# A decoder layer in fp32: three of four query tiles projected and rotated inside the attention steps

## Chip, cores, metric

The kernel runs on one core of one Trainium2 chip. The metric is the device time of one execution in microseconds. The time before is 1650.46 us, the median of 3 runs (1649.22 to 1653.79). Engines are called TensorE (PE, its weight loads PEld), VectorE (DVE), ScalarE (ACT), GpSimd (POOL) and SyncE (SP).

## What is computed

Three sublayers with residuals over x of 4 x 512 x 512, all in fp32. The core of the reference, cut down:

```python
x = x + attn(_layernorm(x), wq, wk, wv, wo, bq, bk, bv)   # 16 heads of 32, 2 kv heads, rope, causal
x = x + mamba(ctx_1024, _layernorm(x), ...)               # scan over 512 steps, 16 states, gated by silu
x = x + ffn(_layernorm(x), Wg, Wu, Wd, Wr, Ag, ...)       # 512 -> 1408 -> 512, top 2 of 8 LoRA experts

q = (x @ wq.T + bq); k = (x @ wk.T + bk); v = (x @ wv.T + bv)
q = apply_rope(q);   k = apply_rope(k)        # [x1*cos - x2*sin, x2*cos + x1*sin]
out = softmax(mask(q @ k.T * scale)) @ v
state = state * exp(d * A) + (d * u) * b      # step of the scan
y = sum_n(state * c)
```

The scan does not need the attention: its input is ctx_1024. Only the gate at its end takes the normalized x.

## The kernel before, in words

The four batches (b, or t for the batch whose feed-forward runs) are worked through one after another, each on one engine program per engine, with semaphores between them. The scan of batch t + 1 is spread over the feed-forward of batch t, the down products of batch t, and the attention of batch t + 1. The order on each engine is written out: `plan` (line 93) lists the scan's 60 pieces on VectorE and which slot each falls into.

For each batch after the first, the slots are: 33 evaluations of the feed-forward (gate and up products, adapters), then 11 slots of the down product, then 32 attention steps (`STEPS`) and four more that only drain. Batch 0 has the 11 slots without down products.

- **Down slot f** on TensorE (lines 970 to 978): 16 matmul records `L974` over the four row tiles, then `project(b, f)`. `projections(f)` (line 131) says what f carries: slots 1 to 5 project the five tiles raw 0 to 4 (0 to 3 are the query tiles of four heads, 4 the keys), slots 2 to 6 rotate them, slot 7 projects the values, slot 8 turns them by transposes.
- **A tile's way**: TensorE projects it with four 128 x 128 by 512 matmuls (each two records in the trace, `L782`) into a bank of `ps_w`; ScalarE adds the bias and moves it to `q_raw[n % 2]` (`L605`), after tile n - 2 has been rotated; TensorE multiplies by a rotation matrix (`L789`); VectorE forms raw * cos + rotated * sin in three operations (`L1105`, `L1108`, `L1112`) and counts `qk_ready`.
- **Attention step s** handles query tile m = s // 8 and row tile i = (s // 2) % 4, two heads of the four. TensorE: scores of s (`L820`, mask `L823`), transposes of the probabilities of s - 2 (`L834`), and at every second step from 5 on the product with the values (`L844`, `L849`). VectorE: maxima (`L1126`), reciprocals, the scan pieces of the step, division (`L1139`). ScalarE: moves of the transposed probabilities (`L637`), exponentials (`L625`), moves of outputs (`L644`), decays for the scan (`L583`). The scores of s wait for the exponentials of s - 2. At steps 31, 33, 34, 35 the output projection `L873` follows.
- **Banks of `ps_w`**: two banks go round by a fixed list of uses (`uses_of`, line 160). `fill` waits until the use before the last is freed.
- **Scan state n**: VectorE multiplies into `state` (`L1086`), scans (`L1091`), multiplies by C (`L1096`); GpSimd then issues a DMA that adds the 1 MB state to y (`L487`), after the add before it has landed. The product of state n waits for the add of state n - 2 (line 1083).
- **Seam**: after the 11 slots VectorE runs `finish` (`L1280`), which empties `ps_a`; the first two scores steps wait for it (`x3_ready`, line 816), and attention waits for all five tiles (line 807).
- **SyncE** loads the context of the next batch after all five tiles of this one are rotated (line 408), then the first weight tiles of the feed-forward.

Of the kernel before, what the change touches and what calls it, by code (L numbers as in the profile page):

```python
# [11 lines left out]
P = 128  # L12
# [118 lines left out]
def projections(f):  # L131


    raw = f - 1 if 1 <= f <= TILES else None
    back = f - 2 if 2 <= f <= TILES + 1 else None
    return raw, back, {TILES + 2: 0, TILES + 3: 1}.get(f)
# [23 lines left out]
def uses_of(first, last):  # L160
# [15 lines left out]
    if not last:  # L176
# [15 lines left out]
def decoder_layer(nc, x, ctx_t, wq, wk, wv, wo, w_in, w_x, w_dt, w_lora, w_r, b_down, a_down, w_tiles, w_adapt, w_down,  # L192
                  vectors, constants, out, bc_rows):
    with ExitStack() as stack:
# [38 lines left out]
        probs_t = [r1[:, 4 + k, :] for k in range(4)] + [xt[:, k, :] for k in range(4)]  # L233
# [3 lines left out]
        r2 = sb("r2", [P, 15, L])  # L237
        k_t, q_t, q_raw, rope_tmp = r2[:, 0, :], r2[:, 8:12, :], r2[:, 12:14, :], r2[:, 14, :]
# [274 lines left out]
        def _(act):  # L513
# [78 lines left out]

            def project(b, f):
                n = projections(f)[0]
                if n is not None:
                    bank = filled(act, ("raw", n), b)
                    if n >= 2:

                        act.wait_ge(qk_ready, b * TILES + n - 1)
                    elif not first_batch(b):  # L600

                        act.wait_ge(down_ready, b)

                    bias = q_bias[:, n:n + 1] if n < MT else vec[:, V_BQ + n:V_BQ + n + 1]
                    nc.scalar.activation(q_raw[:, n % 2, :], ps_w[:, bank, :], ACT.Identity, bias=bias,  # L605
                                         scale=SCALE if n < MT else 1.0).then_inc(work_free[bank], 1)
# [7 lines left out]
            def attention(b, slots):  # L614
# [118 lines left out]
        def _(pe):  # L733
# [39 lines left out]

            def project(b, f):
                raw, back, values = projections(f)
                if raw is not None:
                    if raw == 0:
                        xt_moved("xt", b, False)
                    bank = fill(pe, ("raw", raw), b)
                    for k in range(KT):  # L780
                        w = wq_sb[:, k, raw * P:(raw + 1) * P] if raw < MT else wk_sb[:, k, :]
                        mm = nc.tensor.matmul(ps_w[:, bank, :], w, xt[:, k, :], start=(k == 0), stop=(k == KT - 1))  # L782
                    mm.then_inc(work_full[bank], 1)
                if back is not None:
                    bank = fill(pe, ("back", back), b)

                    raw_bank, raw_count = use(("raw", back), b)
                    pe.wait_ge(work_free[raw_bank], raw_count + 1)
                    nc.tensor.matmul(ps_w[:, bank, :], rot, q_raw[:, back % 2, :], start=True, stop=True)\  # L789
                        .then_inc(work_full[bank], 1)  # L790
# [15 lines left out]
            def attention(b, slots):  # L806
                pe.wait_ge(qk_ready, (b + 1) * TILES)
                pe.wait_ge(v_ready, b + 1)

                def scores(s):  # L810
                    m, i, pair = s // (2 * NT), (s // 2) % NT, s % 2
                    if s >= 2:
# [44 lines left out]
                for s in range(STEPS + 4):  # L857
                    if s < STEPS:
                        scores(s)
                    if 2 <= s < STEPS + 2:  # L860
                        transpose_probs(s - 2)
                    for g in value_groups(s):
# [149 lines left out]
        def _(dve):  # L1012
# [84 lines left out]

            def rotate(b, f):

                total = TILES  # L1100
                _, n, values = projections(f)
                if n is not None:
                    raw_bank, raw_count = use(("raw", n), b)
                    dve.wait_ge(work_free[raw_bank], raw_count + 1)
                    tt(rope_tmp, q_raw[:, n % 2, :], cos_t, ALU.mult).then_inc(rope_chain, 1)  # L1105
                    bank = filled(dve, ("back", n), b)
# [320 lines left out]
```

## Time and profile before

| | |
|---|---|
| profiled execution | 1649.75 us, span 1647.9 us |
| median of the runs | 1650.46 us |
| PE busy | 1406.0 us (85%) |
| DVE busy | 1218.4 us (74%) |
| ACT busy | 604.9 us (37%) |
| POOL busy | 111.9 us (7%) |
| mean granted TensorE clock | 0.876 of full speed |
| chain that ended last | DVE 30%, issue 30%, PE 29%, DMA 6% |

A share is one of the whole span, over stages with different limits; it doesn't say which engine a stage waits for. For that the busy times of single stages and the timeline at their seams have to be read. A granted clock of 1.00 is 2.4 GHz, of 0.50 it is 1.2 GHz. "Issue" as the releaser of a weight load means that TensorE waited for nothing that the profile shows.

### The profile page before, as it was taken

What the parts mean: (1) busy time and instruction counts of PE and PEld (TensorE: products, weight loads), DVE (VectorE), ACT (ScalarE), POOL (GpSimd) and SP (SyncE); (2) the same over time, 40 slices, a digit from 0 to 9 for tenths busy, and PEclk for the clock granted to TensorE, in tenths of its full rate; (3) what the DMA queues carried; (4) which work ended last, traced back from release to release, by engine and by line L of the source; (5) the groups of instructions that cost most, each with busy time, mean ns of one, the idle gap of its engine ahead of it and who ended that gap; (6) DMA issues with size and microseconds to landing.
All of it is one profiled execution on the core that took longest, in us unless ns stands there. A gap on an engine that the chain in (4) does not pass through costs nothing.

```text
span 1647.9 us, 16148 instructions
## 1 busy us (share of the span) xinstructions
PE 1406.0 (85%) x5768; PEld 685.0 (42%) x5768; DVE 1218.4 (74%) x1411; ACT 604.9 (37%) x1436; POOL 111.9 (7%) x116
## 2 busy tenths in 40 slices
PE   5756767999888799899889699899879788799999
PEld 2333433443333354444334255444334345454434
DVE  4899996589989766759998865759998967623330
ACT  5165553323223584232232376242333267211110
POOL 0000001001100000000110000100210000100000
PEclk8855558999999699899999779899999869789999
DMA  4167761123666631112656822012556741101112
GB/s 185 39 147 153 154 141 27 44 66 108 143 141 166 166 66 26 39 50 78 159 128 159 196 68 52 26 37 84 124 131 152 173 135 27 26 13 64 48 32 83
DMA packets 53278, 158.81 MB, mean 96 GB/s; under 512 B 5072, under 2 KB 10704, under 8 KB 44752
## 3 DMA queue, kind: packets, MB, share of 16 engines
q0 software_dynamic: 9216, 67.11, 19.8%
q1 hardware_dynamic: 25664, 54.23, 9.9%
q10 hardware_dynamic: 18320, 36.45, 8.6%
q8 instruction: 47, 0.77, 0.2%
q14 instruction: 31, 0.25, 0.0%
HBM read 86.20 MB, written 4.46 MB: 55 GB/s over the span
## 4 chain that ended last, share of the span: by engine, by line
DVE 30%; issue 30%; PE 29%; DMA 6%; ACT 4%; POOL 2%; DVEq 0%; ACTq 0%; POOLq 0%
DVE state L1091 11%; DMA y_sb<-state 5%; PE ps_a L894 5%; DVE state L1086 4%; PE ps_a L974 4%; PE ps_a L820 3%; DVE state L1096 3%; PE ps_b L834 3%; PE ps_w L873 3%; PE ps_a L906 3%; POOL rstd L477 2%; PE ps_b L914 2%; PE ps_w L782 2%; ACT r L625 2%; DVE neg_max L1126 2%
## 5 line engine op out<-in xcount | busy, mean ns | idle before, releaser
L894 PE MATMUL ps_a<-xt,w_sb 128*128 128x512 f32 x704 | 319.2, 607 | 0.0
L1091 DVE TENSOR_TENSOR_SCAN state<-decay,state 128x2048 f32<-128x2048 f32 x64 | 282.8, 4418 | 5.3 <-ACT decay L583 0.5
L677 ACT ACTIVATE r<-ps_a 128x512 f32<-128x512 f32 x132 | 78.6, 596 | 380.6 <-PE ps_a L906 202.8
L894 PEld LDWEIGHTS ps_a<-xt,w_sb 128*128 128x128 f32 x704 | 138.1, 197 | 174.9 <-issue 174.9
L820 PE MATMUL ps_a<-r 32*128 32x512 f32 (+3 forms) x512 | 140.4, 634 | 81.7 <-ACT r L625 55.2
L906 PE MATMUL ps_a<-r,wb_sb 128*128 128x512 f32 x352 | 177.1, 628 | 35.9 <-DVE r L1267 33.7
L583 ACT ACTIVATE decay<-dt_sb,decay_rate 128x511 f32<-128x511 f32 x256 | 162.9, 712 | 104.9 <-DVE state L1096 72.2
L1260 DVE SCALAR_TENSOR_TENSOR r<-r,ps_a 128x512 f32<-128x512 f32 x132 | 89.9, 681 | 146.3 <-ACT r L677 146.3
L625 ACT ACTIVATE r<-ps_a,neg_max 128x128 f32<-128x128 f32 (+3 forms) x256 | 133.6, 534 | 116.6 <-DVE neg_max L1126 116.1
L974 PE MATMUL ps_a<-wd_sb,r 128*128 128x512 f32 x352 | 162.4, 613 | 0.0
L1086 DVE TENSOR_TENSOR state<-du_sb,bc_sb 128x2048 f32<-128x2048 f32 x64 | 146.3, 2286 | 4.7 <-DMA y_sb<-state 4.6
L1096 DVE TENSOR_TENSOR state<-state,bc_sb 128x2048 f32<-128x2048 f32 x64 | 145.9, 2280 | 0.7
L834 PE MATMUL ps_b<-cst,r 128*128 128x128 f32 x640 | 121.4, 333 | 26.0 <-ACT xt L637 16.8
L906 PEld LDWEIGHTS ps_a<-r,wb_sb 128*128 128x128 f32 x352 | 67.4, 197 | 131.1 <-issue 124.7
L1126 DVE TENSOR_REDUCE neg_max<-ps_a 128x2 f32<-128x256 f32 (+3 forms) x128 | 104.0, 814 | 21.1 <-PE ps_a L823 20.2
L487 POOL DMA_DIRECT2D y_sb<-state x64 | 56.1, 876 | 752.5 <-DVE state L1096 676.9
L974 PEld LDWEIGHTS ps_a<-wd_sb,r 128*128 128x128 f32 x352 | 70.1, 200 | 88.8 <-issue 86.8
L834 PEld LDWEIGHTS ps_b<-cst,r 128*128 128x128 f32 x640 | 89.9, 174 | 34.7 <-issue 29.5
L914 PE MATMUL ps_b<-r,ad_sb 128*128 128x512 f32 x176 | 89.8, 635 | 13.5 <-DVE r L1267 13.5
L820 PEld LDWEIGHTS ps_a<-r 32*128 32x128 f32 x512 | 49.9, 237 | 118.4 <-ACT r L625 77.2
L1267 DVE TENSOR_TENSOR r<-r,ps_a 128x512 f32<-128x512 f32 x132 | 90.7, 687 | 9.6
L477 POOL TENSOR_TENSOR rstd<-var_eps,cst 128x1 f32<-128x1 f32 x48 | 56.0, 1167 | 576.4 <-DVE var_eps L1024 576.4
(120 smaller groups left out, 1475.7 us busy)
## 6 DMA issues: line engine op xcount, KB each, us to landing
y_sb<-state POOLq DMA_DIRECT2D x64, 1024.0 KB, 9.7
bc_sb<-bc_rows ACTq DMA_DIRECT2D x64, 512.0 KB, 5.1
w_sb<-in_w_tiles SPq DMA_DIRECT2D x44, 512.0 KB, 3.7
wd_sb<-in_w_down SPq DMA_DIRECT2D x44, 256.0 KB, 3.5
wb_sb<-in_w_adapt SPq DMA_DIRECT2D x44, 128.0 KB, 2.1
xa<-in_x SPq DMA_DIRECT2D x4, 1024.0 KB, 5.2
out_x<-xb SPq DMA_DIRECT2D x16, 256.0 KB, 7.0
xn_att<-in_ctx_t SPq DMA_DIRECT2D x4, 512.0 KB, 6.1
```

Source lines behind the costliest of these rows:

```text
L583: nc.scalar.activation(decay[:, n % 2, j, 1:L], dt_sb[:, j, 1:L], ACT.Exp, scale=decay_rate[:, j, n:n + 1]).then_inc(decay_ready, 1)
L625: nc.scalar.activation(probs[:, (2 * s + k) % 4, 0:(i + 1) * P], score_place(s, k), ACT.Exp, bias=neg_max[:, s % 2, k:k + 1], accum_out=ro ...
L820: nc.tensor.matmul(score_place(s, k), q_t[rows, m, i * P:(i + 1) * P], k_t[rows, 0:width], start=True, stop=False, tile_position=(rows.sta ...
L834: mm = nc.tensor.transpose(ps_b[:, k, kt * P:(kt + 1) * P], probs[:, (2 * s + k) % 4, kt * P:(kt + 1) * P], ident)
L894: mm = nc.tensor.matmul(ps_a[:, 2 * (f % 2) + half, :], w_sb[:, slot, at + k * P:at + (k + 1) * P], xt[:, k, :], start=(k == 0), stop=Fals ...
L906: mm = nc.tensor.matmul(ps_a[:, 2 * (f % 2) + half, :], wb_sb[:, f % 2, at:at + P], low[:, 2 * half + k - 1, :], start=False, stop=(k == 2 ...
L914: mm = nc.tensor.matmul(ps_b[:, k - 1, :], ad_sb[:, f, :], hk[:, (2 * f + k - 1) % 4, :], start=(f == 0), stop=(f == FT - 1), skip_group_c ...
L974: mm = nc.tensor.matmul(ps_a[:, i, :], hb[:, f, i * P:(i + 1) * P], wd_sb[:, f % 2, :], start=(f == 0), stop=False, skip_group_check=True)
L1086: tt(state[:, n % 2, :, :], du_sb[:], row, ALU.mult).then_inc(scan_chain, 1)
L1091: nc.vector.tensor_tensor_scan(flat, decay[:, n % 2, :, :].rearrange("p j l -> p (j l)"), flat, 0.0, ALU.mult, ALU.add).then_inc(scan_chai ...
L1096: tt(state[:, n % 2, :, :], state[:, n % 2, :, :], row, ALU.mult).then_inc(scan_chain, 1)
L1126: nc.vector.tensor_reduce(neg_max[:, s % 2, :], both, AX.X, ALU.max, negate=True)\
```

## The change

The tile order becomes keys first: tile 0 is the keys, tiles 1 to 4 are the four query tiles. Only tiles 0 and 1 and the values stay in the down slots: projections in slots 1 and 2, rotations in 2 and 3, values in 3 and turned in 4. Tile m + 2 for m = 0, 1, 2 moves into the attention steps of query tile m: its projection stands at step 8m + 1 (after the transposes, ahead of the value product), its rotation matmul at 8m + 3, VectorE's three operations at 8m + 4 ahead of the scan pieces of that step. Scores wait for their own query tile at the start of each m. The number of operations is the same; the plan of the scan pieces isn't touched. Since the normalized and transposed x (`xt`) is now read until step 17, the four buffers of transposed probabilities that lay in it move to `r2[4:8]`.

```diff
 def projections(f):
-    raw = f - 1 if 1 <= f <= TILES else None
-    back = f - 2 if 2 <= f <= TILES + 1 else None
-    return raw, back, {TILES + 2: 0, TILES + 3: 1}.get(f)
+    raw = f - 1 if 1 <= f <= 2 else None
+    back = f - 2 if 2 <= f <= 3 else None
+    return raw, back, {3: 0, 4: 1}.get(f)
+
+
+def late_projections(s):
+    m, at = divmod(s, 2 * NT)
+    if m + 1 >= MT:
+        return None, None, None
+    return [m + 2 if at == k else None for k in (1, 3, 4)]
...
         for s in range(STEPS + 4):
+            raw, back, _ = late_projections(s)
+            names += [("raw", raw)] * (raw is not None) + [("back", back)] * (back is not None)
             names += [("pv", g) for g in value_groups(s)]
...
-        probs_t = [r1[:, 4 + k, :] for k in range(4)] + [xt[:, k, :] for k in range(4)]
+        probs_t = [r1[:, 4 + k, :] for k in range(4)] + [r2[:, 4 + k, :] for k in range(4)]
...
+            def move_raw(b, n):
+                bank = filled(act, ("raw", n), b)
+                if n >= 2:
+                    act.wait_ge(qk_ready, b * TILES + n - 1)
+                    act.wait_ge(v_turned, b + 1)
...
                 if projections(f)[2] == 0:
                     act.wait_ge(v_full, b + 1)
-                    act.wait_ge(qk_ready, b * TILES + TILES)
+                    act.wait_ge(qk_ready, b * TILES + 1)
...
                         exponents(s)
+                        if late_projections(s)[0] is not None:
+                            move_raw(b, late_projections(s)[0])
                     for g in value_groups(s):
                         move_output(g)
...
             def attention(b, slots):
-                pe.wait_ge(qk_ready, (b + 1) * TILES)
                 pe.wait_ge(v_ready, b + 1)
...
+                    if s % (2 * NT) == 0:
+                        pe.wait_ge(qk_ready, b * TILES + m + 2)
...
                     if 2 <= s < STEPS + 2:
                         transpose_probs(s - 2)
+                    raw, back, _ = late_projections(s)
+                    if raw is not None:
+                        project_raw(b, raw)
+                    if back is not None:
+                        rotate_raw(b, back)
                     for g in value_groups(s):
                         weigh_values(g)
...
                     if 1 <= s <= STEPS:
                         invert_sums(s - 1)
+                    if late_projections(s)[2] is not None:
+                        rotate_tile(b, late_projections(s)[2])
                     if s < STEPS:
                         for piece in slots[ATT + s]["dve"]:
                             scan_piece(b, piece)
```

`project_raw`, `rotate_raw` and `rotate_tile` are the bodies of the old code under new names. The context load of the next batch still waits for `qk_ready` of all five tiles, which now comes at step 20 of the attention.

## Rows read from the trace of the kernel before

**Rows 1.** Busy times by stage: window, length, busy us by engine, clock, DMA share.

```profile
81.00:250.00 169.00, 111.44 (x728) 62.76 (x728) 166.94 (x124) 95.07 (x261) 13.30 (x15) 0.58 0.66 146
...
468.00:553.00 85.00, 69.40 (x158) 30.38 (x157) 77.44 (x43) 22.96 (x37) 6.08 (x7) 0.92 0.68 161
...
553.00:650.00 97.00, 89.61 (x825) 52.08 (x826) 61.39 (x102) 63.41 (x213) 3.94 (x5) 0.83 0.32 81
```

**Rows 2.** Timeline of TensorE at the seam: start, us, engine, line, operation, idle before.

```profile
540.83 3.60 PE L981 MATMUL ps_a<-bd_sb,r 128*128 128x512 f32 x8
...
553.47 0.80 PE L820 MATMUL ps_a<-r 32*128 32x128 f32 x4 [9.04 <-DVE xb L1280]
...
653.24 3.60 PE L739 MATMUL ps_w<-xn_att,win_sb 128*128 128x512 f32 x8
```

**Rows 3.** Chain of work that ended last, batch 1: start us, us, what.

```profile
530.99 9.61 DMA y_sb<-state
...
541.21 8.59 DMA y_sb<-state
```

**Rows 4.** Timeline of VectorE, scan pieces and their waits for adds.

```profile
533.02 4.42 DVE L1091 TENSOR_TENSOR_SCAN state<-decay,state 128x2048 f32<-128x2048 f32 x1
...
540.62 2.29 DVE L1086 TENSOR_TENSOR state<-du_sb,bc_sb 128x2048 f32<-128x2048 f32 x1 [0.65 <-DMA y_sb<-state]
...
1310.22 2.29 DVE L1086 TENSOR_TENSOR state<-du_sb,bc_sb 128x2048 f32<-128x2048 f32 x1 [1.18 <-DMA y_sb<-state]
```

**Rows 5.** Chain of work that ended last: one projection, one rotation matmul.

```profile
475.99 3.43 PE ps_w L782 x8
...
486.29 0.87 PE ps_w L789 x2
```

**Rows 6.** Timeline of VectorE in the down stage of batch 1: rotations.

```profile
487.19 0.69 DVE L1108 TENSOR_TENSOR r<-ps_w,cst 128x512 f32<-128x512 f32 x1 [5.34 <-PE ps_w L789]
...
515.32 0.67 DVE L1105 TENSOR_TENSOR r<-r,cst 128x512 f32<-128x512 f32 x1
...
517.41 2.29 DVE L1096 TENSOR_TENSOR state<-state,bc_sb 128x2048 f32<-128x2048 f32 x1
```

**Rows 7.** Page, part 6: DMA issues, KB each, median us to landing.

```profile
wd_sb<-in_w_down SPq DMA_DIRECT2D x44, 256.0 KB, 3.5
```

**Rows 8.** Timeline of VectorE in batch 0 before attention.

```profile
61.06 0.69 DVE L1105 TENSOR_TENSOR r<-r,cst 128x512 f32<-128x512 f32 x1
...
70.35 0.69 DVE L1108 TENSOR_TENSOR r<-ps_w,cst 128x512 f32<-128x512 f32 x1 [3.62 <-PE ps_w L789]
...
81.15 2.28 DVE L1086 TENSOR_TENSOR state<-du_sb,bc_sb 128x2048 f32<-128x2048 f32 x1
```

**Rows 9.** Busy times by window of the attention stage of batch 1.

```profile
553.00:560.00 7.00, 6.28 (x30) 3.38 (x32) 3.75 (x9) 3.47 (x16) 0.00 (x0) 0.50 1.00 250
...
560.00:567.00 7.00, 6.67 (x38) 3.37 (x40) 6.47 (x7) 3.52 (x12) 0.00 (x0) 0.50 0.91 334
...
567.00:575.00 8.00, 7.61 (x36) 3.67 (x38) 3.12 (x6) 6.95 (x19) 0.00 (x0) 0.50 0.00 1
...
575.00:583.00 8.00, 8.00 (x128) 5.81 (x124) 4.90 (x12) 6.96 (x28) 0.86 (x1) 0.94 0.54 120
```

**Rows 10.** Timeline of TensorE and its weight loads as the clock rises.

```profile
464.12 3.78 PE L914 MATMUL ps_b<-r,ad_sb 128*128 128x512 f32 x4 [3.76 <-DVE r L1267]
...
469.40 0.34 PEld L974 LDWEIGHTS ps_a<-wd_sb,r 128*128 128x128 f32 x1 [0.52 <-issue]
...
470.68 0.19 PEld L974 LDWEIGHTS ps_a<-wd_sb,r 128*128 128x128 f32 x1 [0.24 <-issue]
```

**Rows 11.** Timeline of ScalarE in attention step 4 of batch 1.

```profile
566.53 2.55 ACT L583 ACTIVATE decay<-dt_sb,decay_rate 128x511 f32<-128x511 f32 x4
```

**Rows 12.** Timeline of TensorE in the attention of batch 1: waits for ScalarE.

```profile
598.25 0.70 PE L820 MATMUL ps_a<-r 32*128 32x256 f32 x4 [0.95 <-ACT r L625]
...
626.63 1.52 PE L820 MATMUL ps_a<-r 32*128 32x512 f32 x4 [2.70 <-ACT r L625]
```

More of the change, by code:

```diff
@@ L591, in transposed @@
                         .then_inc(work_free[bank], 1)
+            def move_raw(b, n):
[3 more added lines that the diff above has]
+                    act.wait_ge(v_turned, b + 1)
+                elif not first_batch(b):
+                    act.wait_ge(down_ready, b)
+                bias = q_bias[:, n - 1:n] if n > 0 else vec[:, V_BK:V_BK + 1]
+                nc.scalar.activation(q_raw[:, n % 2, :], ps_w[:, bank, :], ACT.Identity, bias=bias,
+                                     scale=SCALE if n > 0 else 1.0).then_inc(work_free[bank], 1)
             def project(b, f):
@@ L595, in project @@
                 if n is not None:
[L596 to L606, printed above, removed]
+                    move_raw(b, n)
                 if projections(f)[2] == 0:
                     act.wait_ge(v_full, b + 1)
-                    act.wait_ge(qk_ready, b * TILES + TILES)
+                    act.wait_ge(qk_ready, b * TILES + 1)
                     nc.scalar.activation(q_raw[:, 0, :], ps_b[:, 0, :], ACT.Identity,
@@ L772, in xt_moved, with project_raw, rotate_raw @@
                     pe.wait_ge(work_free[bank], count + 1)
+            def project_raw(b, n):
+                bank = fill(pe, ("raw", n), b)
+                for k in range(KT):
+                    w = wq_sb[:, k, (n - 1) * P:n * P] if n > 0 else wk_sb[:, k, :]
+                    mm = nc.tensor.matmul(ps_w[:, bank, :], w, xt[:, k, :], start=(k == 0), stop=(k == KT - 1))
+                mm.then_inc(work_full[bank], 1)
+            def rotate_raw(b, n):
+                bank = fill(pe, ("back", n), b)
+                raw_bank, raw_count = use(("raw", n), b)
+                pe.wait_ge(work_free[raw_bank], raw_count + 1)
+                nc.tensor.matmul(ps_w[:, bank, :], rot, q_raw[:, n % 2, :], start=True, stop=True)\
+                    .then_inc(work_full[bank], 1)
             def project(b, f):
@@ L778, in project @@
                         xt_moved("xt", b, False)
[L779 to L783, printed above, removed]
-                if back is not None:
[L785 to L790, printed above, removed]
+                    project_raw(b, raw)
+                if back is not None:
+                    rotate_raw(b, back)
                 if values == 0:
@@ L1096, in scan_piece, with rotate_tile @@
                     tt(state[:, n % 2, :, :], state[:, n % 2, :, :], row, ALU.mult).then_inc(scan_chain, 1)
+            def rotate_tile(b, n):
+                raw_bank, raw_count = use(("raw", n), b)
+                dve.wait_ge(work_free[raw_bank], raw_count + 1)
+                tt(rope_tmp, q_raw[:, n % 2, :], cos_t, ALU.mult).then_inc(rope_chain, 1)
+                bank = filled(dve, ("back", n), b)
+                part = q_t[:, n - 1, :] if n > 0 else k_t
+                tt(part, ps_w[:, bank, :], sin_t, ALU.mult).then_inc(work_free[bank], 1)
+                dve.wait_ge(rope_chain, b * TILES + n + 1)
+                bank, count = use(("back", n), b)
+                dve.wait_ge(work_free[bank], count + 1)
+                tt(part, part, rope_tmp, ALU.add).then_inc(qk_ready, 1)
+                dve.wait_ge(qk_ready, b * TILES + n + 1)
             def rotate(b, f):
-                total = TILES
                 _, n, values = projections(f)
                 if n is not None:
[L1103 to L1106, printed above, removed]
-                    part = q_t[:, n, :] if n < MT else k_t
-                    tt(part, ps_w[:, bank, :], sin_t, ALU.mult).then_inc(work_free[bank], 1)
-                    dve.wait_ge(rope_chain, b * total + n + 1)
-                    bank, count = use(("back", n), b)
-                    dve.wait_ge(work_free[bank], count + 1)
-                    tt(part, part, rope_tmp, ALU.add).then_inc(qk_ready, 1)
-                    dve.wait_ge(qk_ready, b * total + n + 1)
+                    rotate_tile(b, n)
                 if values == 1:
```

2 lines of the change are left out of this document (added).

## Prediction

> **What bounds the kernel now.** I read the busy times by stage first, because the change moves work from one stage to the next one. In batches 1 to 3, which look alike (the rows are of batch 1), a stage of 85 us holds the down products and the projections, and a stage of 97 us holds the 32 attention steps and the output projection [rows 1]. In the down stage VectorE is busy 77 of 85 us, TensorE 69. In the attention stage it is the other way round: TensorE 90 of 97, VectorE 61. Batch 0 is different: it has no down products, and the long scan fills VectorE for 167 of 169 us of its attention stage, with TensorE at 111.
>
> Next, who waits at the seam. TensorE is through with the last product of the down stage, begun at 540.83 and 3.6 us long, and then stands idle 9.04 us until VectorE's first sum of the finish, behind a scan piece that ends at 552.1, lets the first scores go [rows 2]. So the end of the down stage is VectorE's, not TensorE's. A TensorE product taken out of it shortens nothing by itself; a VectorE operation does.
>
> Third, what is late behind VectorE. Every scan state is added to y by a DMA of 1 MB. The add issued at 530.99 lands 9.61 us later, and the next is issued at 541.21, so adds can follow each other every 10 us or so [rows 3]. A state costs VectorE 2.3 + 4.4 + 2.3 = 9.0 us, less small overlaps 8.9 [rows 4, 6]. One state buffer comes free only when the add of two states ago has landed, so with nothing else on VectorE the adds are the slower chain. Where no rotation stands between the pieces this shows already: the product at 540.62 waited 0.65 us for an add, the one at 1310.22 waited 1.18 us [rows 4].
>
> **The change, part by part.**
>
> *Down stage, batches 1 to 3.* TensorE loses three projections of 3.43 us and three rotations of 0.87 us [rows 5], 12.9 us. None of it is on the path that sets the end, by the 9.04 us of idle time. VectorE loses three rotations. One is three operations of 0.68 to 0.69 us, and takes from 515.32 to 517.41, 2.1 us [rows 6]; three are 6.3 us. Slots 0 to 2 are as before (tiles 0 and 1, the first rotation), so the 5.34 us that VectorE waits for that rotation [rows 6] stays. What is late next is the add chain. I replay it: the output product of state 8 ends at 506.9 instead of 509.0, its add lands at 507.2 + 9.5 = 516.7, while VectorE is free at 515.9 (wait 0.8); the adds of states 9 and 10 then land at 526.7 and 536.7 with VectorE free at 525.7 and 535.8 (waits 1.0 and 0.9); the next at 546.0 with VectorE free at 545.8, where the wait is 0.2 to 0.9. The last product ends at 548.8 instead of 552.1: **-3.3 us a batch** of the 6.3. Bounds: -6.3 if adds land a microsecond sooner, -1 if they land later, because TensorE now runs through slots 5 to 10 in 3.43 us each and calls for a 256 KB down tile in each of them; such a load takes 3.5 us in the middle [rows 7]. The Trainium skill ("Trainium Kernel Development and Optimization", Key Constraints) says that DMAs of all issuing queues run on the same 16 engines and interleave; by that the squeezed loads would push the adds towards the -1 end. TensorE itself would be done near 523 and can afford every wait there. The values come in slots 3 and 4 now; they need the first rotation (488.7) and ScalarE, which stands behind the state that VectorE ends at 495.4; VectorE wants them at 504, so nothing waits.
>
> *Batch 0 before attention.* Here VectorE comes from the polynomial at 61.06 and spends 20.1 us until the first scan product at 81.15, a wait of 3.62 us for TensorE among it, since each projection from the third on must wait for a rotation on VectorE [rows 8]. After the change it has two rotations (61.06 to 65.2; the second one's matmul needs nothing of VectorE now), the copy of the values 0.4, the pieces of 2.3 and 2.3 us and a memset: the product starts near 70.5. **-10.6 us**; no add is in flight yet, so nothing is given back. Bounds -8 to -11.
>
> *Batch 0, attention.* VectorE gets the three rotations back, 6.3 us, in an engine that idles 2 us of 169. TensorE has some 58 us of idle time there: of the 169 / 16 = 10.6 us of a pair of steps it works 7.0 us [rows 1]. A projection at the low clock (6.9 us, below) overdraws one pair by about 3 us, which double buffering of the scores takes up in part. **+6.3 and +1** (bounds +5 and +6.3 + 3 x 3 = +15). Batch 0 in all: -3.3.
>
> *Attention, batches 1 to 3.* I take it in three parts, by the granted clock [rows 9]; the tiles come at steps 1 and 3, 9 and 11, 17 and 19, the VectorE part at steps 4, 12 and 20.
> Steps 0 to 7 (553 to 576): the clock is at 1.2 GHz, after 9 us of idle time. The first projection comes at 555.7. Dense products at this clock follow each other every 0.34 + 0.52 = 0.86 us (row of 469.40), so the eight of a projection take 6.9 us, all of it ahead of the next scores. In the down stage such dense work began at 464.12 and ran every 0.43 us from 470.68 [rows 10], so the clock is probably up right after the projection. That gives back 1.9 us of the 3.8 us until the scan piece at 560.12. Beyond it faster matmuls are worth little: ScalarE then holds the chain (maxima behind the scan until 565.4, exponentials, then 2.55 us of decays until 569.1, and only then the next exponentials [rows 11]; busy 6.95 of 8 us). I give 1 us. The rotation's matmul falls in the scan, its VectorE part before 569.1. Sum 6.9 - 1.9 - 1.0 = +4.0.
> Steps 8 to 15 (576 to 592): TensorE is busy 8.0 of 8 us at nearly full clock [rows 9]. All of 3.43 + 0.87 counts, and the value product of step 13 now takes the bank that VectorE's rotation of step 12 frees: by the order about 1 us late, half of it counted. +4.8.
> Steps 16 to 23: the projection follows the transposes of 595.2 under the scan piece, where TensorE waited 0.95 us for ScalarE before it went on at 598.25 [rows 12]: +2.2 there, +0.9 for the rotation, and a dip of the clock from 599.9 to 603.5 (its matmuls take twice the time there, 1.7 us lost), of which I give back half, -0.9. +2.2.
> Sum **+11 us a batch**. Bounds: 6.5 (clock up at once and every idle gap used) and 17 (16.4 us of matmuls, nothing given back, a wait).
> ScalarE's three moves of 0.69 us go from one stage to another without a path of their own, and the probabilities' other buffers cost the same.
>
> *SP's queue.* The context load now waits for the fifth tile (step 20, near 605), and the first two weight tiles and their adapters queue behind it. Their first user starts at 653.24 [rows 2], 45 us later: nothing. The same loads leave the first 14 us of the stage, where the DMA engines are busy 1.00 and 0.91 [rows 9], with no user there.
>
> **Sum.** 3 x (11.0 - 3.3) - 3.3 = +19.8 us. The profiled execution took 1649.75 us (span 1647.9), the median is 1650.46, 0.7 above. 1669.6 for the one, **1670** for the other.
>
> **Rivals.**
> *The clock pays for it (faster, 0.12).* One place: the first projection of each attention stage. At 553 to 575 TensorE is busy 20.6 of 22 us and yet runs at 1.2 GHz, with thin 32-row matmuls and small gaps [rows 9]. If the dense projection lifts the clock and it stays up, half of 14.3 us is saved before 575, 1.7 at 600 and 3.9 of the 7.8 us after 626.6, and two gaps of 0.95 and 2.70 us fill up [rows 9, 12]; 16.4 - 7.1 - 1.7 - 3.9 - 3.6 = +0.1 a batch, in all 3 x (0.1 - 3.3) - 3.3 = -13: 1637. It is faster from the point where the stage grows by less than 4.4 us. For it: the rise after dense work in rows 10. Against: ScalarE and the scan hold steps 4 to 7 [rows 11]. The Trainium skill ("TensorE: Matmul & The Clock Gate", Part 1) states that throttled is the default and activity releases it; the rows at 464 to 470 agree, and it is the rule that speaks for this rival.
> *The adds keep up (0.15).* All 6.3 us of the rotations are gained in the down stage: 1670 - 3 x 3.0 = 1661. Against it stand the two waits in rows 4.
> *Waits for banks (0.18).* At steps 5, 13 and 21 the value product waits until VectorE has used the rotated tile, and behind it queue the next scores; at 2 us in nine places, +18: 1688. For it: VectorE runs the rotation after its maxima and, at steps 3 and 19, after a scan piece of 4.4 or 2.3 us.
> *It comes out even (0.08).* The work fits in the gaps of both stages, the clock gives half: growth of about 4.4 us a batch, 1650.
> The forecast keeps 0.47.
>
> **The numbers.** A measurement of this kernel tells about 0.3% (5 us) from no change. Faster is most of the first rival, 0.11; the even case and edges of others make 0.10; the rest is slower, 0.79. The range for 8 in 10 takes the forecast with its bounds, the adds that keep up and nearly all of the bank waits: 1652 to 1690.
>
> **What would show it.** Down stage of batch 1 shorter by 3.3 us, with waits of scan products for adds at three or four places; TensorE idle some 25 us before the first scores; attention stage 11 us longer, with a granted clock above 0.5 from about 562; the first projection there near 6.9 us, the others 3.43; batch 0 done 3 us sooner. The forecast is wrong if the attention stage grows by less than 4.4 us, or if VectorE's scan in batch 0 shows waits for scores of more than 5 us.

## The result, and the profile after

The changed kernel takes **1670.46 us** (median of 4 runs, 1668.15 to 1671.77). The kernel before, run beside it, takes 1652.12 us (4 runs, 1649.22 to 1653.96). The ratio is 1.0111, with an interval of 1.0089 to 1.0133: slower by 18 us. The profiled execution of after took 1668.15 us, with a span of 1666.4. Of the ten runs of the experiment e7 below, one took 2415 us at a mean granted clock of 0.747; it was disturbed and is left out of every number. Line numbers below are those of the kernel they are read from; the late projection is `L789`, its rotation matmul `L796`, the rotation on VectorE `L1123`, `L1126`, `L1130`, the scan pieces `L1108`, `L1113`, `L1118`.

First the same stages as in [rows 1], by window: batch 0's attention, then the down stage and the attention stage of batch 1.

```profile
68.00:238.00 170.00, 113.73 (x729) 62.02 (x727) 167.46 (x132) 95.35 (x259) 13.32 (x15) 0.63 0.63 144
...
462.00:544.00 82.00, 60.28 (x131) 25.64 (x129) 72.64 (x35) 21.55 (x34) 6.26 (x8) 0.85 0.73 170
544.00:652.00 108.00, 98.37 (x851) 54.77 (x852) 66.87 (x110) 65.55 (x216) 3.96 (x5) 0.88 0.29 71
```

In the down stage VectorE's work falls from 77 to 73 us and TensorE's from 69 to 60. The attention stage takes both up, 98 and 67 us. To see whether the end of a stage moved, I compare the spans by the starts of fixed instructions on VectorE in the two profiled executions. The down stage is counted from the first operation of `weigh_down` (`L1272` in before), which weights the down adapters, to the first sum of the finish; attention steps from the maxima of one step to the maxima of another:

| stretch | before | after | change | forecast |
|---|---|---|---|---|
| VectorE's first rotation to the first scan product, batch 0 | 20.09 | 9.23 | -10.9 | -10.6 |
| first scan product to the down stage (attention and feed-forward), batch 0 | 386.79 | 393.53 | +6.7 | +7.3 |
| down stage (`weigh_down` to finish), batches 1, 2, 3 | 84.10, 83.28, 83.43 | 79.99, 80.35, 80.75 | -9.7 | -9.9 |
| attention steps 0 to 7, batch 1 | 22.35 | 26.24 | +3.9 | +4.0 |
| steps 8 to 15, batch 1 | 19.97 | 25.06 | +5.1 | +4.8 |
| steps 16 to 23, batch 1 | 17.52 | 20.04 | +2.5 | +2.2 |
| maxima of step 24 to those of step 31, batch 1 | 17.65 | 18.22 | +0.6 | 0 |
| attention and feed-forward (finish to the next down stage), batches 1, 2, 3 | 301.05, 301.72, 282.02 | 312.68, 311.47, 294.18 | +33.5 | +33 |

The remaining -1.3 us lies at both ends of the run (VectorE comes out of the polynomial at 59.69 instead of 61.06; the tail is 0.1 longer). Within rounding it all adds up to the +18.5 us of the span. Batches 2 and 3 repeat the steps of batch 1 within 0.3 us. Of the +12.1 us that the 32 steps of batch 1 grow by, 0.4 us come back before its next down stage; in batch 2 it is 1.4 of 11.2, and in batch 3 the rest grows by 1.1 more. In which queue is open.

**The down stage.** VectorE there, the answer to [rows 4] (start, us, engine, line, operation, idle before):

```profile
501.28 2.29 DVE L1108 TENSOR_TENSOR state<-du_sb,bc_sb 128x2048 f32<-128x2048 f32 x1
...
511.53 2.29 DVE L1108 TENSOR_TENSOR state<-du_sb,bc_sb 128x2048 f32<-128x2048 f32 x1 [1.08 <-DMA y_sb<-state]
...
521.13 2.29 DVE L1108 TENSOR_TENSOR state<-du_sb,bc_sb 128x2048 f32<-128x2048 f32 x1 [0.42 <-DMA y_sb<-state]
...
530.72 2.29 DVE L1108 TENSOR_TENSOR state<-du_sb,bc_sb 128x2048 f32<-128x2048 f32 x1 [0.42 <-DMA y_sb<-state]
...
540.23 2.29 DVE L1108 TENSOR_TENSOR state<-du_sb,bc_sb 128x2048 f32<-128x2048 f32 x1 [0.34 <-DMA y_sb<-state]
```

No rotation stands between the pieces any more, and the last four products each wait for an add. Their distance is 9.6 us, where VectorE's own work is 9.1. The chain of waits of after, in the same stretch, is now a chain of adds; in [rows 3] it held two of them.

```profile
501.75 9.76 DMA y_sb<-state
...
512.03 9.07 DMA y_sb<-state
...
521.63 9.06 DMA y_sb<-state
...
531.32 8.89 DMA y_sb<-state
```

An add is issued about 0.5 us after the one before has landed, so with 9.1 us in flight the period is 9.6. Over the whole run the adds rise from 5% of the chain to 10%, as the page of after has it.

```profile
DMA y_sb<-state 10%; DVE state L1113 8%; PE ps_a L916 5%; PE ps_a L996 4%; PE ps_w L789 3%; PE ps_a L837 3%; DVE state L1108 3%; PE ps_b L851 3%; DVE state L1118 3%; PE ps_w L895 3%; PE ps_a L928 2%; POOL rstd L486 2%; DVE neg_max L1148 2%;
```

**The seam and the first attention steps.** TensorE, the answer to [rows 2] and [rows 9]:

```profile
521.64 5.40 PE L996 MATMUL ps_a<-wd_sb,r 128*128 128x512 f32 x8 [2.39 <-DMA wd_sb<-in_w_down]
526.87 3.60 PE L1003 MATMUL ps_a<-bd_sb,r 128*128 128x512 f32 x8
543.87 0.80 PE L837 MATMUL ps_a<-r 32*128 32x128 f32 x4 [13.40 <-DVE xb L1304]
...
545.89 5.73 PE L789 MATMUL ps_w<-xt,wq_sb 128*128 128x512 f32 x8
551.55 0.70 PE L837 MATMUL ps_a<-r 32*128 32x256 f32 x4
```

TensorE's idle time before the scores grows from 9.04 to 13.40 us: what it saves in the down stage it waits away. The first late projection takes 5.66 us until the next scores begin. By window (length, busy us of TensorE, its weight loads, VectorE, ScalarE and GpSimd, granted clock, DMA share, GB/s) the clock rises behind it and falls back once:

```profile
543.00:550.00 7.00, 6.13 (x17) 3.14 (x18) 2.84 (x7) 1.62 (x8) 0.00 (x0) 0.50 1.02 244
550.00:557.00 7.00, 7.00 (x38) 2.99 (x37) 4.17 (x5) 4.06 (x15) 0.00 (x0) 1.00 0.22 81
557.00:564.00 7.00, 3.82 (x29) 1.64 (x29) 5.65 (x8) 4.30 (x11) 0.00 (x0) 0.74 0.00 1
564.00:571.00 7.00, 7.00 (x49) 4.26 (x49) 4.82 (x6) 5.91 (x18) 0.00 (x0) 0.53 0.00 0
...
571.00:583.00 12.00, 12.00 (x127) 6.99 (x126) 5.49 (x13) 7.42 (x27) 0.86 (x1) 1.00 0.58 133
```

The scan piece behind this begins 9.36 us after the first maxima (545.03 to 554.39), where it was 5.49 us before. That is +3.87; the rest of the eight steps lasts as long as before, 16.9 us.

### The profile page after: what moved, and what is told of

Its sections match the earlier page's. It is cut to its first block, busy times and chain, and to the rows that moved or that the text cites. A ratio compares the mean times of both kernels' runs of the same rounds, so it can differ in the third digit from the quotient of the medians.

```text
span 1666.4 us, 16160 instructions
## 1 busy us (share of the span) xinstructions
PE 1396.6 (84%) x5768; PEld 674.5 (40%) x5768; DVE 1220.4 (73%) x1411; ACT 605.3 (36%) x1436; POOL 112.0 (7%) x116
## 4 chain that ended last, share of the span: by engine, by line
PE 30%; issue 28%; DVE 25%; DMA 10%; ACT 3%; POOL 2%; DVEq 0%; ACTq 0%; POOLq 0%
DMA y_sb<-state 10%; DVE state L1113 8%; PE ps_a L916 5%; PE ps_a L996 4%; PE ps_w L789 3%; PE ps_a L837 3%; DVE state L1108 3%; PE ps_b L851 3%; DVE state L1118 3%; PE ps_w L895 3%; PE ps_a L928 2%; POOL rstd L486 2%; DVE neg_max L1148 2%; PE ps_b L936 2%; PE ps_w L866 1%
## 5 line engine op out<-in xcount | busy, mean ns | idle before, releaser
L1113 DVE TENSOR_TENSOR_SCAN state<-decay,state 128x2048 f32<-128x2048 f32 x64 | 283.0, 4421 | 5.7 <-ACT decay L592 0.5
L837 PE MATMUL ps_a<-r 32*128 32x512 f32 (+3 forms) x512 | 130.0, 590 | 99.0 <-ACT r L634 55.6
L996 PE MATMUL ps_a<-wd_sb,r 128*128 128x512 f32 x352 | 169.8, 637 | 26.3 <-DMA wd_sb<-in_w_down 26.3
L1108 DVE TENSOR_TENSOR state<-du_sb,bc_sb 128x2048 f32<-128x2048 f32 x64 | 146.4, 2288 | 11.4 <-DMA y_sb<-state 11.1
L1118 DVE TENSOR_TENSOR state<-state,bc_sb 128x2048 f32<-128x2048 f32 x64 | 146.0, 2281 | 0.7
L851 PE MATMUL ps_b<-cst,r 128*128 128x128 f32 x640 | 114.2, 320 | 27.0 <-ACT r L646 26.7
L646 ACT ACTIVATE r<-ps_b 128x128 f32<-128x128 f32 (+3 forms) x256 | 99.6, 443 | 40.5 <-PE ps_b L851 39.2
L837 PEld LDWEIGHTS ps_a<-r 32*128 32x128 f32 x512 | 46.5, 220 | 137.2 <-ACT r L634 69.2
L851 PEld LDWEIGHTS ps_b<-cst,r 128*128 128x128 f32 x640 | 85.2, 166 | 35.1 <-issue 29.7
```

What stands on the lines that cost most here:

```text
L837: nc.tensor.matmul(score_place(s, k), q_t[rows, m, i * P:(i + 1) * P], k_t[rows, 0:width], start=True, stop=False, tile_position=(rows.sta ...
L851: mm = nc.tensor.transpose(ps_b[:, k, kt * P:(kt + 1) * P], probs[:, (2 * s + k) % 4, kt * P:(kt + 1) * P], ident)
L996: mm = nc.tensor.matmul(ps_a[:, i, :], hb[:, f, i * P:(i + 1) * P], wd_sb[:, f % 2, :], start=(f == 0), stop=False, skip_group_check=True)
L1108: tt(state[:, n % 2, :, :], du_sb[:], row, ALU.mult).then_inc(scan_chain, 1)
L1113: nc.vector.tensor_tensor_scan(flat, decay[:, n % 2, :, :].rearrange("p j l -> p (j l)"), flat, 0.0, ALU.mult, ALU.add).then_inc(scan_chai ...
L1118: tt(state[:, n % 2, :, :], state[:, n % 2, :, :], row, ALU.mult).then_inc(scan_chain, 1)
```

## Experiments

Where no number of runs is given, a time is that of one run, the profiled one.

Two theories stood against each other after the result. By the forecast's, the down stage gives back half of its gain to the adds, and the attention stage pays for the projections on TensorE, with VectorE's rotations almost free. The rival to its second half: VectorE's in-order queue holds the chain too, so the rotations are paid there. A second rival is that the low clock at the head of the attention stage sets the price.

### The adds: e1 and e2

The same edit on the kernel before (e1) and after (e2); the add moves a quarter of the state:

```diff
-                    pool.dma_start(y_sb[:].rearrange("p j l -> p (j l)"),
-                                   state[:, n % 2, :, :].rearrange("p j l -> p (j l)"),
+                    pool.dma_start(y_sb[:, 0:1, :].rearrange("p j l -> p (j l)"),
+                                   state[:, n % 2, 0:1, :].rearrange("p j l -> p (j l)"),
```

> The kernel before, with each add of a scan state to y cut to a quarter of its bytes (three of the four tiles of y are left out of the sum). Theory: before the change the adds limit almost nothing, so the stretch from the first operation of weigh_down to the first of finish in batch 1 goes from 84.1 us to 83.5 (only the 0.65 us wait goes), and the whole kernel loses 2 to 5 us. Rival (adds are felt everywhere, by DMA traffic beside the down tiles): the stretch falls by 2 us or more.

> The changed kernel, with each add of a scan state to y cut to a quarter of its bytes (three of the four tiles of y are left out). Theory: the chain of adds took back what the three rotations had freed. Without it the stretch from weigh_down to finish in batch 1 falls from 80.0 us to 77.5 (84.1 less 6.3 less the wait of 0.65 that the kernel before had), and no scan product waits for an add. Rival (VectorE has other waits there, or the down tiles hold it): the stretch stays at 80.

Measured beside before's 1648.99 us: e1 1637.53, e2 1657.03. The down stages of e1 are 82.01, 82.37 and 82.02 us (before 84.10, 83.28, 83.43), those of e2 77.39, 77.29 and 76.15 (after 79.99, 80.35, 80.75). VectorE in e2 (timeline):

```profile
509.53 2.28 DVE L1108 TENSOR_TENSOR state<-du_sb,bc_sb 128x2048 f32<-128x2048 f32 x1
...
518.61 2.29 DVE L1108 TENSOR_TENSOR state<-du_sb,bc_sb 128x2048 f32<-128x2048 f32 x1
...
527.70 2.28 DVE L1108 TENSOR_TENSOR state<-du_sb,bc_sb 128x2048 f32<-128x2048 f32 x1
...
536.78 2.29 DVE L1108 TENSOR_TENSOR state<-du_sb,bc_sb 128x2048 f32<-128x2048 f32 x1
```

The products follow each other every 9.08 us without a wait. With small adds the change is worth 5.2 us a batch in the down stage (82.1 in e1 to 76.9 in e2, means of three), 1.1 us short of the 6.3 us of three rotations; with full adds it is worth 3.2 (83.6 to 80.4). So the full adds cost before 1.5 us a batch and after 3.4: they are what is late next, and of the gain they take back 2.0 us a batch, where the forecast said 3.0. The pages show the other side of this traffic too: beside the small adds the loads of down tiles take 2.7 us in the middle in e1 and 2.8 in e2, where before has 3.5 and after 4.5. The attention steps of e2 are those of after within 0.4 us in batches 1 and 2. One thing fits no expectation: e1 as a whole gained 11.5 us where 2 to 5 were expected. 4.4 lie in the down stages, 4.4 in the attention and feed-forward of the last batch, the rest is spread; the edit also takes three quarters of the adds' traffic from every other stage, and which part that is was not separated.

### TensorE's projections: e3

```diff
-                for k in range(KT):
+                last = KT - 1 if n < 2 else 0
+                for k in range(last + 1):
```

> The changed kernel, with the projections of query tiles 1 to 3 (the late ones) cut to one of their four matmuls (three quarters of the sum are left out). Theory: TensorE's own time is on the path, so the attention stages of batches 1 to 3 get shorter: 2.57 us for each of the two projections at full clock, less than that for the first (5.5 us become 1.7, but the low clock then lasts longer behind it and takes some 2 to 3 back), 6 us a batch, 1650 us in all. Rival (the banks and VectorE's rotation hold the steps): less than 2 us a batch.

Measured 1651.16 us. The steps of batch 1 take 23.84, 22.07, 19.06 and 18.22 us against 26.24, 25.06, 20.04 and 18.22 of after: -2.4, -3.0, -1.0 and 0. In batches 2 and 3 the first three parts lose 1.5 and 1.6, 2.5 and 2.6, 1.0 and 1.0 us. The down stages are 0.3 to 1.6 us shorter than those of after. TensorE in e3:

```profile
545.97 2.02 PE L790 MATMUL ps_w<-xt,wq_sb 128*128 128x512 f32 x2
547.92 1.22 PE L838 MATMUL ps_a<-r 32*128 32x256 f32 x4
```

The projections are on the path in all three parts. In the first one of batch 1, 3.7 us of matmul (5.66 to 1.95) bring 2.4, because the thin matmuls behind it now run at the low clock, 1.22 us where after has 0.70 (the granted clock from 550 to 557 is 0.74, in after 1.00): the projection pays a third of its price itself, by lifting the clock. In steps 16 to 23 only 1.0 of the 2.6 us that are cut comes through.

### VectorE's rotations: e4

The first and the third of the three operations of a late rotation work on one column:

```diff
+                c = slice(0, L if n < 2 else 1)
+                tt(rope_tmp[:, c], q_raw[:, n % 2, c], cos_t[:, c], ALU.mult).then_inc(rope_chain, 1)
...
+                tt(part[:, c], part[:, c], rope_tmp[:, c], ALU.add).then_inc(qk_ready, 1)
```

> The changed kernel, with the first and third of VectorE's three rotation operations of the late tiles cut from 512 columns to one (those tiles are not rotated properly), 1.2 us less on VectorE for each tile. Theory: in batch 0, where VectorE is the bound, 3.6 us are gained; in the attention stages of batches 1 to 3 VectorE has room, and each is within 1 us of the changed kernel's; in all 1664 to 1668 us. Rival (value products wait for the bank that the rotation frees, and TensorE's order passes it on): 1.2 us for each tile, 3.6 a batch, 1656.

Measured 1655.05 us: it is the rival's number. The steps of batch 1 take 25.81, 23.82, 18.97 and 17.58 us, so -0.4, -1.2, -1.1 and -0.6; the stretch of batch 0 from the first scan product on gets 3.5 us shorter, where three rotations of 1.03 us instead of 2.10 save VectorE 3.2. VectorE in steps 12 and 13, in after:

```profile
583.28 0.96 DVE L1148 TENSOR_REDUCE neg_max<-ps_a 128x2 f32<-128x768 f32 x1
584.16 0.15 DVE L1153 RECIPROCAL row_inv<-row_sum 128x2 f32<-128x2 f32 x1
584.23 0.67 DVE L1123 TENSOR_TENSOR r<-r,cst 128x512 f32<-128x512 f32 x1
584.82 0.68 DVE L1126 TENSOR_TENSOR r<-ps_w,cst 128x512 f32<-128x512 f32 x1
585.60 0.69 DVE L1130 TENSOR_TENSOR r<-r 128x512 f32<-128x512 f32 x1
586.33 0.96 DVE L1148 TENSOR_REDUCE neg_max<-ps_a 128x2 f32<-128x768 f32 x1
```

and in e4:

```profile
580.67 0.96 DVE L1149 TENSOR_REDUCE neg_max<-ps_a 128x2 f32<-128x768 f32 x1
...
582.65 0.96 DVE L1149 TENSOR_REDUCE neg_max<-ps_a 128x2 f32<-128x768 f32 x1
```

The maxima of step 13 follow those of step 12 after 3.05 us in after, 1.98 us in e4; in before it was 0.94 (585.29 to 586.23). The exponentials of step 13 need these maxima, and the scores of step 15 and the transposes need the exponentials. TensorE in after:

```profile
585.55 0.43 PE L861 MATMUL ps_w<-cst,row_inv 128*32 128x128 f32 x8 [0.36 <-DVE r L1126]
...
588.61 1.13 PE L837 MATMUL ps_a<-r 32*128 32x512 f32 x4 [0.48 <-ACT r L634]
```

The first wait is the one for the bank that the forecast looked at; the second, for the exponentials, ends last, and e4 has neither. So what is queued behind the rotation on VectorE, the maxima, carries its price into the chain. That it is the maxima and not the bank is read from these rows; no run took the one away without the other.

How much it is shows in the four steps that hold the rotation. Steps 12 to 15 take 11.65 us in before, 13.05 in after and 11.98 in e4, steps 20 to 23 take 9.52, 10.90 and 9.83, in all three batches within 0.02 us. The 1.07 us that e4 cuts from a rotation come through whole, but the whole rotation of 2.1 us costs at most the 1.4 us by which these steps grew: its first 0.7 us fit in.

In steps 0 to 7 the rotation costs nothing: steps 4 to 7 of batch 1 take 12.53 us in before, 12.54 in after and 12.53 in e4. The maxima of step 5 are late there too (3.03 us behind those of step 4, 1.96 in e4), but either way VectorE then waits for ScalarE, which has 2.55 us of decays to do first. VectorE in after, and then in e4:

```profile
565.24 0.29 DVE L1161 TENSOR_TENSOR r<-ps_w,r 128x128 f32<-128x128 f32 x1 [2.45 <-ACT r L653]
...
562.79 0.29 DVE L1162 TENSOR_TENSOR r<-ps_w,r 128x128 f32<-128x128 f32 x1 [3.51 <-ACT r L653]
```

The 0.4 us that e4 gains in the first eight steps lie ahead of the rotation.

### The clock at the seam: e5 and e6

Dummy matmuls, 512 columns each, behind the last product of the down stage, so that TensorE arrives at the high clock: nine in the kernel before (e5), fourteen in after (e6).

```diff
+                if b is not None:
+                    for _ in range(9):
+                        nc.tensor.matmul(ps_b[:, 1, :], rot, cos_t, start=True, stop=True)
```

> The kernel before, with nine 512-column products of constants put on TensorE after the last product of each down stage (batches 1 to 3), into a bank that nobody reads: 7.7 us of the 9 us in which it stands idle before the first scores. Theory of the forecast (the low clock at the head of the attention stage costs little, since ScalarE and the scan hold steps 4 to 7): steps 0 to 7 go from 22.4 to 19.5 us, 3 us a batch, about 9 us in all. Rival (the low clock costs half of TensorE's busy time there): steps 0 to 7 go to about 14 us, 24 us in all. If the clock falls back with the first thin matmuls, nothing is gained.

> The changed kernel with fourteen such products in the 13.4 us of idle time before the first scores. The first late projection then runs at full clock, 3.43 us instead of 5.5. Theory: steps 0 to 7 go from 26.2 to about 23.5 us, the rest stays, so 2.7 us a batch. Rival (clock counts in full): 20 us or less.

e5: 1648.52 us (median of 10 runs, 1635.83 to 1656.93) against 1651.99 (19 runs), ratio 0.9974 with an interval of 0.9944 to 1.0004: no difference that can be told. The profiled execution is one of the longer ones, 1655.85 us. Its windows in the attention of batch 1, as [rows 9], and then that of steps 8 to 15 of batch 2:

```profile
553.00:560.00 7.00, 4.85 (x26) 2.47 (x27) 4.18 (x10) 3.98 (x16) 0.00 (x0) 0.70 0.99 221
560.00:567.00 7.00, 7.00 (x40) 3.60 (x39) 6.69 (x6) 3.15 (x13) 0.00 (x0) 0.50 0.99 347
...
961.00:986.00 25.00, 23.56 (x230) 15.04 (x232) 14.39 (x22) 16.43 (x54) 0.86 (x1) 0.77 0.29 65
```

The first scores still run at the high clock, 0.49 us where before has 0.80, but the third take 1.22 us as in before. The clock is 0.70 for the first 7 us and then 0.50 all the same, although TensorE works 14.3 of the next 15 us. Steps 0 to 7 last 22.34, 21.67 and 22.18 us in the three batches, 0 to 0.9 less than before. The trial brought something else to light. In batches 2 and 3 the clock was low in steps 8 to 15 too (0.77 and 0.71; before has 0.98 and 0.93 in the same windows), and there the steps took 25.19 and 24.49 us instead of 20.41 and 20.65. So a low clock costs about 4 to 5 us in these steps. What a high one would be worth through all of steps 0 to 7 stays unmeasured, since the dummies did not bring it about.

e6: 1665.12 us; steps 0 to 7 take 25.68, 25.66 and 27.37 us against 26.24, 25.99 and 26.14 of after. TensorE in e6:

```profile
546.17 0.49 PE L837 MATMUL ps_a<-r 32*128 32x128 f32 x4 [2.99 <-DVE xb L1307]
...
547.82 5.35 PE L789 MATMUL ps_w<-xt,wq_sb 128*128 128x512 f32 x8
```

The projection still takes 5.3 us. The granted clock was 1.00 up to 545 and 0.76 in the window of 545 to 552. The scores right behind the gap of 2.99 us still take 0.49 us, so the clock fell behind them, and of the projection's eight records four last about 1.06 us and four 0.6: it ran half at either level. The price of a projection wholly at 2.4 GHz in this place was therefore not measured; in steps 8 to 15 it is contained in the +5.1 us.

### Both halves apart: e7 and e10

The late projections in batch 0 only; in batches 1 to 3 all five tiles are projected and rotated in the down slots, as before (but keys first):

```diff
-def projections(f):
+def projections(f, b):
+    if b > 0:
+        raw = f - 1 if 1 <= f <= TILES else None
+        back = f - 2 if 2 <= f <= TILES + 1 else None
+        return raw, back, {TILES + 2: 0, TILES + 3: 1}.get(f)
...
-def late_projections(s):
+def late_projections(s, b):
     m, at = divmod(s, 2 * NT)
-    if m + 1 >= MT:
+    if b > 0 or m + 1 >= MT:
         return None, None, None
```

> The change in batch 0 alone; in batches 1 to 3 all five tiles are projected and rotated in the down slots, keys first. Theory: the two halves of the change have opposite signs; batch 0 keeps its 4 us (11 gained before attention, 7 given back in it) and the other batches are as before: 4 us faster than before, 1648. Rival (the 5.5 us by which the first weigh_down comes earlier are mostly the start of the run): within 1 us of before.

> The kernel of e7 again, for a trace. Theory: before attention of batch 0 the two rotations, values and pieces take 9.2 us as in the changed kernel (20.1 before), its attention is 6.7 us longer than before, and batches 1 to 3 show the stage times of the kernel before within 1 us: 84 us of down stage, 22.4, 20 and 17.5 us for eight steps each.

e7: 1648.23 us (median of nine runs) against 1651.99, ratio 0.9977 with an interval of 0.9968 to 0.9987, so -3.8 us; the forecast's term for batch 0 was -3.3. e10 is the same kernel, run for its trace: 1648.79 us. There VectorE goes from the first rotation (60.86) to the first scan product (70.09) in 9.2 us, and batch 0 from the product to the down stage takes 396.08 us, +9.3 (where after has +6.7), of which 2 us lie behind the last maxima (219.99 against 218.08). Down stages and attention steps of batches 1 to 3 are those of before within 1.3 and 0.8 us. The rest of the change, in batches 1 to 3, is thus worth 1670.46 - 1648.23 = +22 us by medians; the forecast had 3 x 7.7 = +23.

### Another place for the projections: e8

```diff
-    return [m + 2 if at == k else None for k in (1, 3, 4)]
+    at = {2: (3, 5, 6), 3: (9, 11, 12), 4: (15, 17, 18)}
+    return [next((n for n in at if at[n][k] == s), None) for k in range(3)]
```

> The changed kernel with other places for two late tiles: tile 2 projected at step 3, rotated at 5 and 6; tile 4 at step 15, 17 and 18, both beside a scan piece of 4.4 us, in which TensorE stands idle 1 to 3 us; tile 3 as in the change. Theory: part of each projection is hidden there, 1.5 us a batch for tile 4 and up to 2 for tile 2, if the clock stays as it is: 1660 to 1666. Rival (place doesn't matter, each microsecond of TensorE counts): within 3 us of 1670.

Measured 1663.31 us. The first eight steps of the three batches take 24.43, 25.39 and 24.98 us instead of 26.24, 25.99 and 26.14; the first projection now runs while VectorE scans. Later groups of eight steps gain up to 1.2 us and twice lose 0.5 or 0.6; the whole stays 11 us above before's 1651.99. Of the two places tried neither makes the projections free, in a stage where TensorE is busy 98 of 108 us.

### A better use of the seam: e9

In the down stage VectorE waits 5.34 us in its queue for the first rotation's matmul [rows 6], with scan pieces behind it that need nothing of it. e9 keeps the late projections in batch 0, as e7, and in batches 1 to 3 lets VectorE rotate each tile one slot later:

```diff
                 _, n, values = projections(f, b)
+                if b > 0:
+                    n = projections(f - 1, b)[1]
```

> The kernel of e7 (the change in batch 0 alone), and in the down slots of batches 1 to 3 VectorE rotates each tile one slot later (slots 3 to 7), so that it no longer stands 5.3 us before the first rotation matmul. Theory: VectorE's own order sets the end of the down stage while its states take longer than an add (about 10 us); with the rotations still between them they do, so nearly all of the 5.3 us are gained, 4 to 5 a batch: weigh_down to finish 79.5 us, the kernel near 1635. Rival (the adds are the floor of the stage as in the changed kernel): 82 us a stage or more, 1644 or more.

Measured **1631.72 us** (median of 4 runs, 1628.02 to 1632.53) against 1650.14 (7 runs, with those of e10): ratio 0.9875 with an interval of 0.9853 to 0.9897. VectorE in its down stage of batch 1:

```profile
484.59 0.69 DVE L1126 TENSOR_TENSOR r<-r,cst 128x512 f32<-128x512 f32 x1
485.19 0.68 DVE L1129 TENSOR_TENSOR r<-ps_w,cst 128x512 f32<-128x512 f32 x1
485.98 0.69 DVE L1133 TENSOR_TENSOR r<-r 128x512 f32<-128x512 f32 x1
488.18 2.29 DVE L1111 TENSOR_TENSOR state<-du_sb,bc_sb 128x2048 f32<-128x2048 f32 x1 [1.51 <-DMA y_sb<-state]
...
542.60 2.29 DVE L1111 TENSOR_TENSOR state<-du_sb,bc_sb 128x2048 f32<-128x2048 f32 x1 [0.73 <-DMA y_sb<-state]
```

The wait of 5.3 us is gone and the adds ask 1.5 and 0.7 us of it back. Down stages are 80.32, 79.06 and 79.35 us: as short as those of after, with all five rotations still in them and nothing added to the attention steps (22.35, 20.11, 17.54, 17.60 in batch 1). Against e10 that is -10.7 us in the down stages (2.5, 4.2 and 4.0; the expectation was 4 to 5 each); -5.5 us more lie in the attention and feed-forward stretches of all batches, of which no single row shows the cause. It beats both kernels, by 18 and by 39 us.

## Why the prediction was right, and which steps were not

The forecast of 1670 us and the measured 1670.46 agree a little better than they should: the change is +18.3 us where +19.8 were forecast, and before was 1.7 us slower beside after than when it was forecast from. The agreement is not by cancelling alone, for each of the eight stretches of the table comes out within 0.6 us of its term. But that is agreement of sums. Each mechanism behind them has its own verdict.

- **What bounds the two stages.** Right. TensorE's saving in the down stage turned into idle time (9.04 to 13.40 us), VectorE's was worth 3.2 of 6.3 us a batch.
- **The adds are late next.** Right, by the waits of four products and by e2, where they vanish with the small adds. The replay put the waits at 0.8, 1.0, 0.9 and at most 0.9 us; they are 1.08, 0.42, 0.42 and 0.34. The sentence on shared DMA engines (the Trainium skill, "Trainium Kernel Development and Optimization", Key Constraints) pointed to slower adds. The traces agree that the transfers press on each other (down loads of 2.8 us in e2, 4.5 in after), but it was the down loads that paid, 4.5 us instead of 3.5, while the adds in this chain took 8.9 to 9.8 us, and the median over the run is 9.7, as in before.
- **TensorE idle some 25 us before the first scores.** Wrong: 13.40. The forecast let TensorE run through the slots in 3.43 us each and be done near 523; it ended at 530.5, mostly since three down tiles came late (4.21, 1.72 and 2.39 us in batch 1, 26.3 us in ten waits over the run). The loads take 4.5 us in the middle where [rows 7] has 3.5. The forecast said that TensorE could afford such waits, and it could. (A slot is 8 matmul records, 3.43 us, as the forecast has it, and not the 16 of the kernel's description.)
- **Batch 0.** Right on both sides, -10.9 and +6.7 us, and e7 shows their sum by itself, -3.8. The single trace of e10 has +9.3 for the second, so that side is known to some 3 us only.
- **First projection 6.9 us, 1.9 given back until the scan, 1.0 beyond.** The sum of 4.0 held, its terms did not all. The projection took 5.66 us, because the clock rose within it; 1.8 us came back until the scan piece, as forecast; beyond it nothing did. A term that was 1.2 too high and one that was 1.0 too good cancel.
- **The rotation's price.** This is the step that failed. The forecast gave VectorE's rotations 0.5 us in steps 8 to 15, for a bank, and nothing in steps 16 to 23. e4 shows that a rotation shorter by 1.07 us shortens either part by 1.1 to 1.2, through the maxima behind it, and the growth of steps 12 to 15 and 20 to 23 bounds the whole price at 1.4 us each. The sum held since TensorE's share was put too high. Steps 8 to 11 hold the projection and the rotation's matmul, 4.3 us by the forecast; they grew by 3.7, 3.1 and 3.0 us in the three batches. Steps 16 to 19 were to grow by 2.2 + 0.9 - 0.9 us and grew by 1.1. These errors cancel, and that is luck. Looking at the maxima of the next step on the same queue would have shown it: in an in-order queue the first thing to ask of an inserted operation is what stands behind it.
- **Steps 24 to 31** carry no late work, and still grow by 0.6 us; in e4 this is gone (17.58), in e3 it is not. The cause is open.

Of the rivals, **the clock pays** did not come: half of its condition was met. The clock rose with the first projection (1.00 from 550 to 557) and again from 571, but fell to 0.74 and 0.53 between, after TensorE had waited 2.77 us for exponentials whose maxima stood behind the scan. The forecast, too, had expected it above 0.50 from about 562. The clock gave back 1.8 us until the scan piece, where the rival counted 7.1 before 575, and in steps 16 to 23, where it was 1.00 instead of 0.90, the stage still grew by 2.5. **The adds keep up** fell with the four waits. **Waits for banks** had the right engine and the wrong object; the waits for banks over the whole run are one row of the list of waits (total us, times, longest), 6.7 us and not 18:

```profile
PE ps_w L861 <- DVE r L1126: 6.7, 8, 2.4
```

**It comes out even** wanted a growth of 4.4 us a batch; it was 11.

## What to carry to other kernels

Before moving work from one stage to the next, name for each engine it uses whether that engine sets the end of the stage it leaves and of the stage it enters: here only the rotations counted in the first, while in the second most of the projections and two thirds of two of the three rotations counted. Then ask what is late next where time is freed (here adds of 1 MB every 9.6 us), and what is queued behind each inserted operation. A long wait in an in-order queue with unrelated work behind it was here a better target than the work itself: rotating one slot later won in e9 as much as moving three rotations out of the stage did, and cost nothing elsewhere.

## What the runs showed of the hardware

- TensorE arrived from nine dense matmuls in e5 and ran its first scores at the high level, and the granted clock was still 0.70 and then 0.50 in the next windows, with 32-row matmuls; in after one dense projection, begun at the low level, was followed by a window at 1.00.
- One kernel spreads widely: the ten runs of e5 lie between 1635.83 and 1656.93 us. In its profiled run steps 8 to 15 of two batches, with a low clock, took 8.6 us more than in before; the runs' mean granted clock goes the same way, 0.879 to 0.882 at 1655.8 to 1656.9 us and 0.891 to 0.893 at 1637.8 to 1635.8. In which steps the short runs had the clock was not seen, as they left no trace.
- An add of 1 MB within the chip's memory takes 9.7 us (median) from issue to landing, in before and after, and in the down stage of after the next is issued 0.5 us later. An add of a quarter of that takes 5.8 us (e1, e2), not a quarter of the time. Beside the small adds the loads of 256 KB take 2.7 and 2.8 us, beside the full ones 3.5 and 4.5.
